# Perceiver block, one core: key rows loaded from SBUF to SBUF, batch 0 prepared alone first, chunks 4 to 7 between the first score units, all squarings in units 64 to 112

## The reference

```
x = x + xattn(layernorm(x), ctx, ctx, mask)     # 16 heads of 8 dimensions
x = x + ssm(layernorm(x))                       # W_in and W_out divided by max(largest singular value, 1), gated scan over 128 tokens
x = x + ffn(layernorm(x))                       # weights binarised as mean(|w|) * sign(w), hidden 512, GELU
```

## Time and profile before

| | us |
|---|---|
| median of 3 runs | 327.06 |
| profiled execution, time | 329.18 |
| its span (first to last instruction) | 327.4 |
| TensorE busy | 257.0 (79%) |
| VectorE busy | 231.3 (71%) |
| ScalarE busy | 200.7 (61%) |
| GpSimd busy | 108.2 (33%) |
| transfers | 34.48 MB, mean 105 GB/s |

### The profile page before, as it was taken

One profiled execution on the slowest core, in us unless ns is written; L12 is line 12 of the kernel. 1 busy time (PEld: TensorE's weight loads), 2 busy tenths in 40 slices (PEclk: granted clock), 3 DMA queues, 4 the chain that ended last, 5 costly groups with the idle time before them and its releaser, 6 DMA issues.

```text
span 327.4 us, 9590 instructions
## 1 busy us (share of the span) xinstructions
PE 257.0 (79%) x3904; PEld 160.6 (49%) x3904; DVE 231.3 (71%) x425; ACT 200.7 (61%) x309; POOL 108.2 (33%) x267
## 2 busy tenths in 40 slices
PE   0799615499999999999999999999999877550276
PEld 0577401245555556555565655555655444440156
DVE  4358839267878788787878989879888940538941
ACT  1267700267777777877777777777876665195042
POOL 7123421115434553345433665232113120104210
PEclk9999955569999999999999999999999996785559
DMA  6926979941535415344263312311321000000001
GB/s 146 381 88 220 226 179 292 363 153 50 148 92 153 146 50 161 107 127 145 52 188 102 103 50 77 73 50 50 80 68 52 3 4 2 0 0 0 0 0 32
DMA packets 24565, 34.48 MB, mean 105 GB/s; under 512 B 2444, under 2 KB 19112, under 8 KB 24392
## 3 DMA queue, kind: packets, MB, share of 16 engines
q1 hardware_dynamic: 23716, 33.37, 35.0%
q0 software_dynamic: 128, 0.14, 0.5%
q10 hardware_dynamic: 676, 0.33, 0.3%
HBM read 20.20 MB, written 13.63 MB: 103 GB/s over the span
## 4 chain that ended last, share of the span: by engine, by line
PE 58%; ACT 17%; SPq 6%; DMA 6%; DVE 6%; issue 5%; POOL 2%; POOLq 0%; ACTq 0%; DVEq 0%
PE ps L447 15%; ACT probs L739 13%; PE ps L434 13%; PE ps L418 6%; PE ps L320 4%; PE ps L357 4%; SPq L259 4%; PE ps L487 3%; PE ps L495 3%; DMA k_rows_dram<-k_parts 2%; DMA w_kv<-in_L_xattn_Wq_dram 2%; PE ps L455 2%; PE ps L667 2%; PE ps L340 2%; DMA ctx_buf<-in_ctx_dram 1%
## 5 line engine op out<-in xcount | busy, mean ns | idle before, releaser
L1191 DVE TENSOR_REDUCE pmax<-ps 128x2 f32<-128x1024 f32 x128 | 156.1, 1224 | 42.8 <-PE ps L418 41.0
L739 ACT ACTIVATE probs<-ps 128x1024 f32<-128x1024 f32 x128 | 130.8, 1022 | 47.2 <-PE ps L434 47.2
L447 PE MATMUL ps<-probs,v_now 128*9 128x128 f32 x2048 | 82.4, 280 | 0.2 <-ACT probs L739 0.2
L434 PE MATMUL ps<-q_max,k_rows 51*128 51x128 bf16 x1024 | 52.3, 223 | 13.9 <-ACT probs L739 12.8
L447 PEld LDWEIGHTS ps<-probs,v_now 128*9 128x9 f32 x2048 | 43.8, 91 | 34.9 <-issue 33.1
L418 PE MATMUL ps<-k_rows,q_now 48*128 48x512 bf16 x256 | 51.2, 398 | 11.0 <-DMA k_rows<-k_rows_dram 8.3
L968 POOL CAST max_cols<-negmax 128x2 bf16<-128x2 f32 x32 | 6.1, 192 | 133.6 <-DVE negmax L1197 133.6
L434 PEld LDWEIGHTS ps<-q_max,k_rows 51*128 51x128 bf16 x1024 | 30.0, 96 | 37.5 <-ACT probs L739 22.7
L418 PEld LDWEIGHTS ps<-k_rows,q_now 48*128 48x128 bf16 x256 | 12.8, 96 | 14.2 <-DMA k_rows<-k_rows_dram 8.5
L690 ACT ACTIVATE ctxT<-ps 128x512 f32<-128x512 f32 x16 | 9.6, 597 | 14.2 <-PE ps L320 14.2
L357 PE MATMUL ps<-power 128*128 128x128 f32 x96 | 16.7, 297 | 0.2 <-DVE power L1119 0.2
(11 more groups left out here) (184 smaller groups left out, 360.0 us busy)
## 6 DMA issues: line engine op xcount, KB each, us to landing
k_rows<-k_rows_dram SPq DMA_DIRECT2D x64, 192.0 KB, 3.3
k_rows_dram<-k_parts SPq DMA_DIRECT2D x16, 384.0 KB, 3.8
ctx_buf<-in_ctx_dram SPq DMA_DIRECT2D x16, 256.0 KB, 5.5
k_rows_dram<-k_parts SPq DMA_DIRECT2D x16, 256.0 KB, 3.7
k_rows_dram<-k_parts SPq DMA_DIRECT2D x16, 128.0 KB, 4.1
mask_sb<-in_mask_1x1xSxS_ff_dram SPq DMA_DIRECT2D x1, 1024.0 KB, 9.3
q_all<-q_rows_dram SPq DMA_DIRECT2D x2, 384.0 KB, 6.5
w_nat<-in_L_ffn_w_dram SPq DMA_DIRECT2D x2, 256.0 KB, 8.8
```

The lines of the kernel that those rows point to most:

```text
L434: t = pe.matmul(dst, k_rows[rows, i % 4, at:at + P], q_max[rows, i % 2, :], start=not masked, stop=True, skip_group_check=masked)
L447: t = pe.matmul(ps[at:at + HEAD_COLS, 6, 0:P], v_now[:, i % 2, 4 * c + j, HEAD_COLS * h:HEAD_COLS * h + HEAD_COLS], probs[:, c, h, P * j:P ...
L739: act.activation(probs[:, u % CHUNKS, :, :], ps[:, 4:6, :], ACT.Exp).then_inc(probs_ready, 1)
L1191: dve.tensor_reduce(pmax[:, i % 2, :, c], ps[:, bank:bank + 2, :], AX.X, ALU.max).then_inc(pmax_ready, 1)
```

## The change

Key rows are loaded from the key parts in SBUF straight into `k_rows`, six DMAs a pair. The triangular six blocks become seven, since the two copies of three parts are read as they lie; a head has 56 rows. Queries are stored and loaded in two rounds (batch 0, then the rest), and TensorE and VectorE read `q_all` and `v_all` directly. Only chunks 0 to 4 are prepared before the first scores; chunks 5 to 7 lie between scores 2 and 5, and the parts of chunks 4 to 7 are made by GpSimd. All 24 squarings lie in units 64 to 111, four in each eight, renormalised each fourth time. Weight means and signs move to units 42 and 44 of VectorE. Context buffers go from 8 to 6.

```diff
-SQ_PERIOD = 3
-TINY = 1e-30
+SQ_PERIOD = 4
+TINY = 1e-36
...
+    CTX_SLOTS = 6
...
-    K_GROUPS = ((0, 3), (3, 2), (5, 1))
-    BLOCKS = 6
-    ROWS = HD * BLOCKS
+    TRIPLE = HD * PARTS
+    ROWS = 2 * TRIPLE + HD
...
-    LOADS = 32
+    LOADS = 16 * 6
...
+        def load_half_pair(eng, i, h):
+            b, p = divmod(i, PAIRS)
+            at, slot = HALF_ROWS * h, i % 4
+            heads = slice(16 * p + HD * h, 16 * p + HD * h + HD)
+            keys = slice(KEYS * b, KEYS * b + KEYS)
+            for rows, parts in ((slice(at, at + TRIPLE), PARTS), (slice(at + TRIPLE, at + 2 * TRIPLE), PARTS),
+                                (slice(at + 2 * TRIPLE, at + ROWS), 1)):
+                eng.dma_start(k_rows[rows, slot, :], k_parts[heads, 0:parts, keys]).then_inc(k_rows_loaded[slot], 16)
+
+        def store_q(eng, tok):
+            for part in range(2):
+                eng.dma_start(q_wide[part, :, :, tok], q_parts[:, part:part + 1, tok].broadcast_to(
+                    (P, PARTS, tok.stop - tok.start))).then_inc(once("q_stored"), 16)
+            eng.dma_start(q_last[:, tok], q_parts[:, 2, tok]).then_inc(once("q_stored"), 16)
...
+            def load_pair(i):
+                wait(sp, keyscores_ready, CHUNKS * (i - 3))
+                for h in range(2):
+                    load_half_pair(sp, i, h)
+
+            first_tokens, rest_tokens = slice(0, T), slice(T, TOK)
+            sp.wait_ge(once("q_parts_ready"), 1)
+            store_q(sp, first_tokens)
+            for n in range(CTX_SLOTS, FIRST):
+                load_ctx(n)
+            sp.wait_ge(once("q_stored"), 16 * 3)
+            sp.wait_ge(once("q_all_zeroed"), 1)
+            for h in range(2):
+                load_q(sp, h, slice(0, 1), first_tokens, once("q_loaded"))
+            sp.wait_ge(once("k_ones_ready"), 1)
+            sp.wait_ge(k3_ready, EARLY)
+            load_half_pair(sp, 0, 0)
+            for i in range(1, 4):
+                load_pair(i)
+            sp.dma_start(w1_nat[:, :, :], w1.rearrange("(a p) d -> p a d", p=P)).then_inc(ld["mlp"], 16)
+            sp.dma_start(w2_nat[:, :], w2).then_inc(ld["mlp"], 16)
+            sp.wait_ge(once("q_parts_ready"), 2)
+            store_q(sp, rest_tokens)
             sp.dma_start(w_nat[:, W_IN, :], W_in).then_inc(ld["ssm"], 16)
             sp.dma_start(w_nat[:, W_OUT, :], W_out).then_inc(ld["ssm"], 16)
...
+            sp.wait_ge(once("q_stored"), 32 * 3)
+            for h in range(2):
+                load_q(sp, h, slice(1, B), rest_tokens, once("q_rest_loaded"))
+            load_ctx(FIRST)
+            load_ctx(FIRST + 1)
...
+                sp.wait_ge(k3_ready, CHUNKS * (i // PAIRS + 1))
                 load_pair(i)
-                if i >= 6 and i % 2 == 0 and FIRST + i // 2 - 3 < ALL_CHUNKS:
-                    store_k(FIRST + i // 2 - 3)
+                if i % 2 == 1 and FIRST + 4 + (i - 5) // 2 < ALL_CHUNKS:
+                    load_ctx(FIRST + 4 + (i - 5) // 2)
...
+            def early_chunk(n):
+                pe.wait_ge(ctxT_ready, n)
+                turn_ctx(7, n)
+                pe.wait_ge(k32_ready, n - EARLY)
+                project_k(6, n)
+                wait(pe, v_ready, n - 1)
+                project_v(4 + n % 2, n)
+
             def attend(masked):
-                for u in range(6):
-                    scores(u, masked)
+                scores(0, masked)
+                scores(1, masked)
+                pe.matmul(ps[:, 7, T:TOK], kvT[:, 2, :], xnT[:, T:TOK], start=True, stop=True
+                          ).then_inc(once("q_done"), 1)
+                scores(2, masked)
+                pe.wait_ge(once("q_step"), 5)
+                early_chunk(5)
+                scores(3, masked)
+                early_chunk(6)
+                scores(4, masked)
+                early_chunk(7)
+                scores(5, masked)
                 pe.wait_ge(once("out_bank_zeroed"), 1)
...
+            act.wait_ge(once("k_ones_ready"), 1)
+            act.wait_ge(k3_ready, EARLY)
+            load_half_pair(act, 0, 1)
+            act.wait_ge(once("xn_turned"), 2)
+            copy(xnT[:, T:TOK], ps[:, 3, T:TOK], once("qT_ready"))
+            for n in range(EARLY, FIRST):
+                copy_ctx(7, n)
+                whole_k(n)
+                take_vall(4 + n % 2, n)
...
-            for n in range(FIRST):
-                third(n)
...
+            third(0)
+            third(1)
+            rest_root()
+            third(2)
+            third(3)
...
+                if u == 1:
+                    split_q_first(7, rest_tokens, 4)
+                elif u == 3:
+                    split_q(rest_tokens, 4)
+                elif u == 4:
+                    split_q_rest(rest_tokens, 4)
...
+                elif u == 42:
+                    weight_means()
+                elif u == 44:
+                    weight_signs()
```

More of the change, by code:

```diff
@@ L241, in _ @@
             load_ctx(0)
[L242 to L247, removed]
+            sp.dma_start(w_kv[:, 0, :], Wk).then_inc(ld["wk"], 16)
+            for n in range(1, EARLY):
                 load_ctx(n)
+            sp.dma_start(w_kv[:, 1, :], Wv).then_inc(ld["wv"], 16)
@@ L249, in _ @@
             sp.dma_start(mask_sb[:, :], mask.rearrange("a b q k -> (a b q) k")).then_inc(ld["mask"], 16)
[L250 to L261, removed]
+            for n in range(EARLY, CTX_SLOTS):
+                load_ctx(n)
@@ L388, in _, with turn_xn @@
-            project_k(FIRST - 1)
-            project_v(FIRST - 1)
-            sum_norms(EARLY_SQUARES // SQ_PERIOD)
-            pe.wait_ge(once("q_step"), 1)
-            pe.wait_ge(once("mask_abs_ready"), 1)
-            turn(ps[0:1, 1, 0:P], mask_abs[:, 0:1]).then_inc(once("mask_turned"), 1)
+            def turn_xn(first, n):
+                for i in range(first, first + n):
+                    t = turn(ps[:, 3, P * i:P * i + P], xn[:, i, :])
+                t.then_inc(once("xn_turned"), 1)
@@ new lines, in _ @@
+            turn_ctx(1, 3)
+            pe.wait_ge(r1_ready, 1)
+            project_k(4, 2)
+            pe.wait_ge(ld["wq"], 16)
+            turn(ps[:, 2, P:2 * P], w_kv[:, 2, :])
+            pe.wait_ge(ld["wv"], 16)
+            turn(ps[:, 2, 2 * P:3 * P], w_kv[:, 1, :]).then_inc(once("qv_turned"), 1)
+            pe.wait_ge(once("xn_ready"), 1)
+            turn_xn(0, 1)
+            pe.wait_ge(r1_ready, 2)
+            project_k(5, 3)
+            pe.wait_ge(once("qT_ready"), 2)
+            pe.matmul(ps[:, 2, 0:P], kvT[:, 2, :], xnT[:, 0:T], start=True, stop=True).then_inc(once("q_done"), 1)
@@ new lines, in _ @@
+            project_v(6, 0)
+            project_v(7, 1)
+            pe.wait_ge(v_ready, 1)
+            project_v(6, 2)
+            pe.wait_ge(v_ready, 2)
+            project_v(7, 3)
+            pe.wait_ge(once("mask_abs_ready"), 1)
+            turn(ps[0:1, 0, 0:P], mask_abs[:, 0:1]).then_inc(once("mask_turned"), 1)
+            pe.wait_ge(once("xn_ready"), B)
+            turn_xn(1, B - 1)
+            pe.wait_ge(v_ready, 4)
+            turn_ctx(7, 4)
+            pe.wait_ge(v_ready, 3)
@@ L500, in side_prep @@
                     side_turns(i)
+                elif n == ALL_CHUNKS - 2:
+                    pe.wait_ge(v_half_ready, 2 * m + 2)
+                    pe.wait_ge(ld["ssm"], 32)
+                    for w in range(2):
+                        t = pe.matmul(ps[:, 7, P * w:P * w + P], w_nat[:, w, :], w_nat[:, w, :], start=True, stop=True)
+                    t.then_inc(sq_done, 1)
+                elif n == ALL_CHUNKS - 1:
+                    pe.wait_ge(v_half_ready, 2 * m + 2)
+                    sum_norms(0)
             def turn_vectors():
@@ new lines, in _ @@
+            first_k(0)
+            copy_ctx(0, 2)
+            first_k(1)
+            copy_ctx(1, 3)
+            first_k(2)
+            act.wait_ge(once("qv_turned"), 1)
+            copy(kvT[:, 2, :], ps[:, 2, P:2 * P], once("vec_ready"))
+            copy(kvT[:, 1, :], ps[:, 2, 2 * P:3 * P], once("qT_ready"))
+            act.wait_ge(once("xn_turned"), 1)
+            copy(xnT[:, 0:T], ps[:, 3, 0:T], once("qT_ready"))
+            first_k(3)
+            for n in range(EARLY):
+                take_vall(6 + n % 2, n)
@@ L752, in side_prep @@
                     act.wait_ge(k_done, FIRST + 2 * m + at - 1)
-                    wait(act, split_k_step, 4 * (m - 1))
+                    act.wait_ge(split_k_step, 4 * (m + 1))
                     half = slice(256 * (at - 2), 256 * (at - 2) + 256)
-                    act.activation(k_32[:, n % 2, half], ps[:, 7, half], ACT.Identity, bias=vec[:, BK:BK + 1]
+                    act.activation(k_32[:, n % 4, half], ps[:, 7, half], ACT.Identity, bias=vec[:, BK:BK + 1]
                                    ).then_inc(k32_ready, 1)
+                elif at == 7 and n == ALL_CHUNKS - 2:
+                    act.wait_ge(sq_done, 1)
+                    for dst, s in ((gram[:, :, :], once("gram_ready")), (power[:, 0, :, :], pow_ready)):
```

(1 more changed line is left out.)

521 lines of the change are left out of this document (225 added, 296 removed).

## The result

The changed kernel took 368.84 us (median of 4 runs, 368.12 to 369.84) against 326.10 for the kernel before (median of 4): a ratio of 1.131, 95% interval 1.1243 to 1.1377. The profiled execution has a span of 366.5 us against 327.4. Forecast were 379 us, and the case in which the loads bound.

What follows compares the result with a forecast made beforehand. Key-row loads on one queue were taken as the bound at 8.5 us a pair: pair 4 lands at 78.7, pair 31 231.9 later at 310.6, plus 69.0 gives 379.6, predicted as 379 us; range 320 to 392.

Steps and rivals of the forecast that it cites:

- The rate of the loads: Key-row loads from 8 neighbouring partitions: 54 GB/s, 4.25 us a half, 8.5 us a pair, against 6.5 us of cover.
- The path mechanism: Reads from SBUF: sixteen paths of 27 GB/s shared by neighbours; if four share one, eight partitions reach two.
- The sum: Steady state to end: pair 4 issued near 67.8, pair 31 landed at 310.6, then 69.0 more; span 379.6 us.
- case A: Key-row loads bound the kernel at 8.5 us a pair: 379 us, own range 350 to 392, chance 0.62.
- The start: Before the steady state: key parts complete near 25, scores at 31 to 32, chunk 8 landed near 64 to 65.
- B: Rival: key-row loads stay hidden and the start decides; 325 us, own range 318 to 331, chance 0.26.
- case C: Rival: loads hidden but no earlier start, the queue holding chunk 8 until 64; 330 us, chance 0.12.
- Its term for chunk 8: Start with hidden loads: context chunk 8 issued at 55.3 and landed at 59.7, a gain of 4.3 us.
- The term for the weights' operations: Weight means and signs on VectorE at units 42 and 44: 0 to 1.5 us, taken as 0.8.
- The squarings and what goes with them: One more squaring in each of six groups, +1.4 us; Gram, copies and a sum in units 55 to 63, 0.3.

Runs made afterwards that it cites:

- the run with the spread operations: Weights' means and signs placed singly at units 44 to 54, on the kernel with reordered keys and context chunks 8 and 9 loaded ahead; 319.26 us, ratio 0.9752.
- the run with the step of 12: Changed kernel with each key-row read taking its 8 source partitions 12 apart instead of neighbouring, giving scores of mixed heads; 331.47 us, ratio 1.0154.
- the cheap bias: Changed kernel with reordered key dimensions, right rows read 4 partitions apart, bias bk loaded whole and reordered by one VectorE copy; 331.06 us, ratio 1.0128.

## Why the prediction was right, and its sizes off

**The rate of the loads.** This step carried the forecast, and it held: the loads bound, TensorE's scores waited for them 22 times (1.05 us in the mean, where some 2 were forecast, and 2.0 at the longest), and the mean was 59 GB/s from 200 to 220 us. The path mechanism that was inferred from two rows is shown by the packets at 618, 311 and 159 ns. One step of it was not in those rows: that four neighbours share a path was put in as an if. Forty-eight rows in fours are twelve groups, and eight paths come out only if groups far apart share one, which no row of before shows. The three packet times bear it out afterwards.

The size was 8.5 us a pair; measured were 7.8. A half alone at 54 GB/s would take 4.25, and measured are 3.9. The packet records show the difference: from 100 to 285 us a fifth of the packets took under 400 ns, in 49 bunches where there are some 46 halves. That is the seam at which one half ends and the next begins; that the two use paths of their own there would explain the short packets.

**The sum.** Pair 4 was issued at 70.53, not 67.8; pair 31's scores ran at 299.60, not 310.6; behind them were 66.9 us, not 69.0. The mis-sized terms are 27 x 0.7 = 19 us too much for the pairs, and 4 x (2.0 - 0.6) = 5.6 too little for the context chunks, which wait in the same queue. With +2.7 for the issue of pair 4 and -2.1 for what follows pair 31 these make the 13 us between 379.6 and 366.5 us of span. The total is nearer than its largest term, since the errors have different signs, and that is luck. The ends of case A's own range do not follow from its sum: 7.3 us a pair gives 347, not 350, and 8.9 gives 390, not 392.

**The start.** Key parts were complete near 25 by the forecast and at 23.7 by the trace, and GpSimd did make its root between the second and third of them. Scores came at 34.88, not at 31 to 32: ScalarE was held for 4.69 us by three issues, where 1.5 stood in the sum, and from their end to the first scores it took 6.4 us, where 4.9 stood. In the run with the spread operations, whose reads are short, the same three issues took 2.35 us, so slow reads lengthen them; but ScalarE's own queue held nothing else by then, so what they waited for is not shown. Chunk 8 was issued at 60.73 (forecast 61) and turned at 66.66 (64 to 65): it took 5.9 us from issue to turn, and which traffic held it was not looked for.

**Cases B and C.** The forecast of 325 for hidden loads failed: measured were 331. Its term for chunk 8 is the one that failed: issue at 55.3 and turn at 59.7, where the run with the step of 12 has 56.33 and 62.39 and that with the cheap bias turns it at 63.16. That is nearly the 64 of case C, and its 330 is nearly the time. The term for the weights' operations was 0.8 us; 3.7 were to be had there. The squarings and what goes with them were 1.7, and can be read from the pace behind unit 58: before, the instructions of the maximum's line up to 150 us are

```profile
L1191 DVE TENSOR_REDUCE pmax<-ps x59: 1214/1226/1227, 48.7 to 149.8; 128x2 f32<-128x1024 f32 x59
```

and with the cheap bias

```profile
L1216 DVE TENSOR_REDUCE pmax<-ps x58: 1209/1226/1227, 35.4 to 149.2; 128x2 f32<-128x1024 f32 x58
```

The last maximum starts at 263.6 before and at 266.5 there: 113.8 / 69 = 1.65 against 117.3 / 70 = 1.68 us a unit, 70 x 0.027 = 1.9 us. That term was right within its error. These two rows show also how little the early start leaves: 13.3 us ahead at the first maximum, and one unit behind at 150 us.

## What to carry to other kernels

Ask of a transfer inside the chip which partitions it touches, not only how many bytes it moves: a layout that spreads the rows of one read over eight paths instead of two cost one small copy here and was worth 38 us. Ask of a queue what is behind it: in a kernel bound by one queue every other saving vanishes (0.6 of 14.1 us), so the bound has to go first and the small edits be timed after it. And price work that is moved beside a busy engine by the idle time that it finds there between two steps (1.68 - 1.23 = 0.45 us a unit here), not by the engine's mean idle share.

## What the runs showed of the hardware

- 4 KB packets between partitions of SBUF had medians of 618, 311 and 159 ns for eight neighbours, a step of 16 and a step of 12 or 4; with eight packets in flight 159 ns are 8 x 4096 / 159 = 206 GB/s, and 618 ns are 53. With some fifteen in flight from eight neighbours (GpSimd's queue) it was 54.
- The same issue of a key load took 0.67 us at the median with a step of 12, and 1.10, at most 2.8, with neighbours. The engine that issues is held for it: ScalarE for 4.69 us with three.
- Idle time of 2.3 us in 10 of TensorE at full clock was followed in one execution by a mean clock of 0.66 over the next 10 us; in another, with 1.3 and 1.8 us idle in two such stretches, the clock stayed at 1.00. Both have the weights' operations in the same place.
- Four transfers of 32 single elements put the load behind them off so far that the kernel took 5 us more.
